# Where the router's slots, one power and the last 24 row scatters stand at the end of attention

## The chip, the cores and the metric

One core of a Trainium2 chip runs the whole layer. Its engines are TensorE (PE, matrix products), VectorE (DVE), ScalarE (ACT), GpSimd (POOL) and SyncE (SP, which issues loads and stores). Each works through its own program in order and waits on semaphores for the others. The metric is the device time of one execution in microseconds (us), the median of several runs.

## What is computed

A layer norm, linear attention, a residual sum, a second layer norm, and a mixture of experts with two of eight experts for each token, with a second residual sum. Of 8192 tokens (4 sequences of 2048) with 256 columns each:

```python
q = elu(x @ Wq + bq) + 1; k = elu(x @ Wk + bk) + 1; v = x @ Wv + bv      # 16 heads of 16
# for each position: s += k^T v; z += k; value = (q s) / (q z + 1e-6)
x = x + values @ Wo + bo
logits = einsum('th,eh->te', layernorm(x), router_w)
topk_logits, topk_idx = top_k(logits, 2); probs = softmax(topk_logits)
hmid = gelu(einsum('th,efh->etf', layernorm(x), w1) + b1)
y = einsum('etf,ehf->eth', hmid, w2) + b2
x = x + einsum('eth,te->th', y, combine)                                # combine holds probs
```

## The kernel before

**Blocks of attention.** The positions are cut into 16 blocks (STEPS) of 128, each for all four sequences. An iteration c works on several blocks at once: the front (projections and features) of block c, the attention of block c-1 (flag `bk`), the residual, second norm and router logits of block c-2 (flag `ro`), and the sending of the rows of block c-3 to the experts (flag `sc`). Iteration 16 (c == STEPS) has no front any more: it holds the attention of block 15, the last one. Iterations 17 and 18 have neither front nor attention. Iteration 17 closes the norm of block 15 and sends block 14; iteration 18 sends block 15.

**Sending rows.** For each token two rows of 260 numbers (1040 bytes: the normalised row, token number, two probabilities, first expert) go to `expert_in` in memory, at the row numbers in `cur`, its slots. `row_data` and `router_slots` make them on VectorE (L1405 to L1428); the last write to `cur` raises `slot_done`. GpSimd sends them with `scatter_one(b, t)` (L1801): one indirect DMA for 128 tokens of sequence b and choice t, 8 for a block. `scatter(b)` sends two. Blocks with even numbers count in the semaphore `scat_out[0]`, odd ones in `scat_out[1]`, 16 for each scatter that has landed, 128 for a block.

**The second norm.** `norm_moments` (VectorE, L1244) raises `ln2_ve`; GpSimd's `rstd` (L1769) takes the power -0.5 and raises `ln2_rs`; `norm2_shift` and `router_logits` on VectorE wait for that. In iterations up to 15 the moments come behind residual(r, 3), the slots behind score_lo(0, 3), and each of GpSimd's scatters stands alone between other work. In iteration 16 row_data stands ahead of attention(0), the moments behind state_part(0), the slots behind score_lo(1, 3), and GpSimd issues 2 scatters between state_add(0) and state_add(1) and 6 between state_add(2) and state_add(3).

**After attention.** VectorE adds up the experts' counts (`base`) and makes a table of tiles (`table`, L1632 to L1706, semaphore `tab`). SP then reads the table and loads the first tile's rows (`xg`, L556). The first loads wait for all scatters of even blocks, and of odd blocks only for those before block 15 if the first expert already has 1024 rows; the load of tile 4 (c == PRE) waits for all of them and for the padding rows that ScalarE sends (L1182). Meanwhile SP loads the second layer's weights, `w2raw`, in 8 loads of 512 KB, each behind the landing of the one before it. In the expert part TensorE turns the rows (L897), makes the hidden layer (pS, pO, pA) and the second layer (pU, pF); VectorE puts the result in `yt`, and GpSimd adds it to `out` with two scatters with addition for each tile (L1933). Those of one of the first tiles wait until those of the tile before have landed.

## Time and profile before

| | before |
|---|---|
| median of 3 runs | 1002.96 us |
| lowest, highest | 1000.09, 1008.81 us |
| profiled execution, time | 1012.54 us |
| profiled execution, span | 1010.8 us |
| PE, DVE busy share of the span | 91%, 74% |
| ACT, POOL busy share | 67%, 65% |
| mean granted TensorE clock | 0.973 of full speed |

The profiled execution is one run of its own: its time is 1.7 us more than its span, and 9.6 us above the median of the timed runs. Attention takes the span up to about 560 us, the expert part begins at about 595 us.

### The profile page before, as it was taken

The numbers are of one execution on the slowest core, as the hardware profiler recorded it, in microseconds if no ns is written. First come the engines' busy times: TensorE is split into PE (matmuls) and PEld (weight loads), VectorE is DVE, ScalarE is ACT, GpSimd is POOL, SyncE is SP. The second block draws the span as 40 slices with busy tenths as digits, with TensorE's granted clock in tenths as the row PEclk, the third lists the DMA queues.
The fourth block names the chain that finished last, engine by engine and source line by source line (L and its number), as shares of the span: only waits on it lengthen the run. The fifth ranks groups of instructions, "written<-read, shape, count | busy, mean of one in ns | idle before, by whom it ended". The sixth has DMA issues, their size and how long they took to land. (4 is left out here: it accounts for less than half of the span.)

```text
span 1010.8 us, 33673 instructions
## 1 busy us (share of the span) xinstructions
PE 917.7 (91%) x10722; PEld 739.2 (73%) x10723; DVE 753.0 (74%) x2280; ACT 674.2 (67%) x1295; POOL 652.9 (65%) x580
## 2 busy tenths in 40 slices
PE   6799899999999999999987569899999999999994
PEld 3577677767777777767766247678999999999994
DVE  6788698888898898888886565456666666666663
ACT  8868788888888988898874334444555555555552
POOL 3245868798788888898873444446565555656565
PEclk9999899999999999999999679999999999999998
DMA  6626744554556444644442654345555555555554
GB/s 181 205 74 193 247 137 152 176 159 142 153 156 185 130 151 147 181 154 138 143 143 88 200 179 76 64 80 87 99 87 95 93 92 97 89 99 89 98 87 50
DMA packets 103159, 131.31 MB, mean 130 GB/s; under 512 B 15120, under 2 KB 89360, under 8 KB 102736
## 3 DMA queue, kind: packets, MB, share of 16 engines
q1 hardware_dynamic: 74912, 92.54, 32.9%
q0 software_dynamic: 25680, 35.01, 18.7%
q10 hardware_dynamic: 2464, 2.38, 0.7%
q8 instruction: 64, 1.05, 0.5%
q14 instruction: 39, 0.32, 0.1%
HBM read 64.29 MB, written 65.60 MB: 129 GB/s over the span
## 5 line engine op out<-in xcount | busy, mean ns | idle before, releaser
L1933 POOL DMA_INDIRECT out<-yt,to_token x135 | 213.2, 1579 | 181.4 <-DVE yt L1760 81.8
L1285 DVE SCALAR_TENSOR_TENSOR ahl<-pS,ahl 128x512 f16<-128x512 f32 x240 | 161.4, 683 | 25.3 <-ACT ahl L992 22.3
L992 ACT ACTIVATE ahl<-pS 128x512 f16<-128x512 f32 x240 | 143.0, 603 | 45.2 <-PE pS L663 42.5
L1805 POOL DMA_INDIRECT expert_in<-xn,cur x128 | 131.4, 1027 | 35.9 <-issue 24.5
L1201 ACT ACTIVATE g<-pS,b1s 128x256 f32<-128x256 f32 (+1 forms) x140 | 57.2, 461 | 92.0 <-PE pS L573 92.0
L659 PE MATMUL pS<-cbs 128*128 128x384 bf16 x240 | 79.5, 331 | 21.9 <-DVE ahl L1285 17.7
L573 PE MATMUL pF<-xT,was 128*128 128x512 f16 x384 | 93.0, 379 | 6.1 <-DVE xT L1290 6.0
L573 PE MATMUL pS<-gT,w1s 128*128 128x256 f16 (+1 forms) x840 | 97.4, 272 | 1.2 <-issue 1.1
L1726 DVE TENSOR_TENSOR ghl<-g,ghl 128x1024 f16<-128x1024 f32 (+1 forms) x68 | 83.0, 1220 | 20.5 <-ACT ghl L1228 16.0
L573 PE MATMUL pF<-w2s,ghl 128*128 x816 | 95.4, 273 | 2.4 <-issue 1.6
L573 PE MATMUL pU<-w2s,ghl 128*128 x804 | 94.1, 273 | 1.8 <-issue 1.4
L663 PE MATMUL pS<-qst,kst 128*128 128x256 f16 x480 | 92.1, 274 | 0.0
L1799 POOL TENSOR_TENSOR state<-state,ut 128x272 f32<-128x272 f32 x64 | 49.8, 779 | 65.1 <-DVE ut L1324 64.3
L573 PEld LDWEIGHTS pS<-gT,w1s 128*128 x840 | 81.0, 99 | 13.0 <-issue 2.3
L684 PE MATMUL pO<-vhl,ahl 128*128 128x17 f16 x3072 | 87.8, 171 | 2.8 <-DVE ahl L1285 2.8
L684 PEld LDWEIGHTS pO<-vhl,ahl 128*128 128x128 f16 x3072 | 85.0, 96 | 6.0 <-DVE ahl L1285 3.8
L573 PEld LDWEIGHTS pF<-w2s,ghl 128*128 128x128 f16 x816 | 79.4, 98 | 13.0 <-issue 3.4
L573 PEld LDWEIGHTS pU<-w2s,ghl 128*128 128x128 f16 x804 | 78.2, 98 | 12.3 <-issue 2.8
L1201 ACT ACTIVATE g<-pO,b1s 128x256 f32<-128x256 f32 (+1 forms) x72 | 29.1, 458 | 77.9 <-PE pO L573 75.8
L1228 ACT ACTIVATE ghl<-g 128x1024 f16<-128x1024 f32 (+1 forms) x68 | 72.0, 1059 | 0.1
L573 PEld LDWEIGHTS pF<-xT,was 128*128 128x128 f16 x384 | 36.0, 98 | 40.4 <-DVE xT L1290 7.8
L663 PEld LDWEIGHTS pS<-qst,kst 128*128 128x128 f16 x480 | 47.2, 98 | 18.8 <-issue 0.5
(223 smaller groups left out, 2180.3 us busy)
## 6 DMA issues: line engine op xcount, KB each, us to landing
xg<-expert_in SPq DMA_DIRECT2D x64, 260.0 KB
qk_parts<-qkhl SPq DMA_DIRECT2D x64, 256.0 KB, 2.3
qst<-qk_parts SPq DMA_DIRECT2D x192, 64.0 KB
kst<-qk_parts SPq DMA_DIRECT2D x96, 128.0 KB
xs<-x SPq DMA_DIRECT2D x16, 512.0 KB, 4.7
out<-x SPq DMA_DIRECT2D x16, 512.0 KB, 3.2
w1raw<-w SPq DMA_DIRECT2D x16, 256.0 KB
w2raw<-w SPq DMA_DIRECT2D x8, 512.0 KB
```

What stands on the lines that cost most here:

```text
L573: mm = nc.tensor.matmul(out, lhs(a, k), rhs(b_, k), start=(t == 0), stop=(t == len(terms) - 1))
L659: nc.tensor.matmul(o[:].rearrange("p (h q) -> p h q", q=C)[:, :, 0:STACK], ident16, mask_first, start=True, stop=False, skip_group_check=True)
L663: mm = nc.tensor.matmul(o[:, e * 2 * C:(e + 1) * 2 * C], kst[:, sp_, pr, b * C:(b + 1) * C], qst[:, sp_, :, pr, b * C:(b + 1) * C], start= ...
L684: mm = nc.tensor.matmul(pO[:, h * VC:(h + 1) * VC], ahl[:, b % 2, a, h * C:(h + 1) * C], vhl[:, sp_, b_, b, h * VC:(h + 1) * VC], start=False,
L992: nc.scalar.activation(ahl[:, b % 2, 0, n * 4 * C:(n + 1) * 4 * C], score_bank(fr, n)[:], ACT.Relu).then_inc(sc_hi, 1)
L1201: nc.scalar.activation(g[:, p1, f, h * P:h * P + width], hidden[p1][f // 2][:, c0:c0 + width], ACT.Gelu, bias=b1s[:, bass.ds(e * FC + f, 1 ...
L1228: nc.scalar.activation(ghl[:, p1, 0, :, 0:n], g[:, p1, :, 0:n], ACT.Copy).then_inc(g_hi, 1)
L1285: V.scalar_tensor_tensor(ahl[:, b % 2, 1, cols], score_bank(fr, n)[:], 0.0, ahl[:, b % 2, 0, cols], ALU.max, ALU.subtract).then_inc(sc_lo, 1)
L1726: V.tensor_tensor(ghl[:, p1, 1, :, 0:n], g[:, p1, :, 0:n], ghl[:, p1, 0, :, 0:n], ALU.subtract).then_inc(g_lo, 1)
L1799: G.tensor_tensor(sb_, sb_, ut[:, b % 2], ALU.add).then_inc(state_new, 1)
L1805: G.indirect_dma_start(xg_dram, bass.IndirectOffsetOnAxis(ap=cur[:, qp, 2 * b + t:2 * b + t + 1], axis=0), xn2[:, qp, b], None).then_inc(s ...
L1933: G.indirect_dma_start(out, bass.IndirectOffsetOnAxis(ap=to_token[:, c % 2, s:s + 1], axis=0), yt[:, c % 2, s], None, compute_op=ALU.add). ...
```

## The change

Four edits. On VectorE, row_data, norm_moments, router_slots and norm2_shift of iteration 16 go to where the other iterations have them. On GpSimd, iteration 16 sends its 8 scatters singly between the state additions. In iteration 17, the power of block 15 (`rstd`) goes ahead of the first scatter of block 14. And of the last 16 scatters (blocks 14 and 15) each pair waits until the pair before it has landed.

```diff
-                if sc and c not in (STEPS, STEPS + 1):
+                if sc and c != STEPS + 1:
                     row_data()
...
-                if ro and c not in (STEPS, STEPS + 1):
+                if ro and c != STEPS + 1:
                     norm_moments(r, st2, mv2, ve2, (ln2_st, ln2_mv, ln2_ve))
...
-                if sc and c not in (STEPS, STEPS + 1):
+                if sc and c != STEPS + 1:
                     router_slots()
-                if ro and c not in (STEPS, STEPS + 1):
+                if ro and c != STEPS + 1:
                     norm2_shift()
...
-                if c == STEPS:
-                    row_data()
                 if bk:
                     attention(0)
                     state_part(0)
-                if c == STEPS:
-
-                    norm_moments(r, st2, mv2, ve2, (ln2_st, ln2_mv, ln2_ve))
...
-                if c == STEPS:
-                    router_slots()
-                    norm2_shift()
...
+                    if c > STEPS and t == 0 and b:
+
+                        pool.wait_ge(scat_out[qp], 128 * qh + 32 * b)
+                    if c > STEPS and t == 0 and b == 0:
+
+                        pool.wait_ge(scat_out[1 - qp], 128 * ((q + 1) // 2))
...
+                last = sc and c == STEPS
                 single = sc and c < STEPS
...
-                if c == STEPS + 1:
-                    scatter_one(0, 0)
                 if ro:
                     rstd(r, ve2, rs2, ln2_ve, ln2_rs)
                 if c == STEPS + 1:
-                    scatter_one(0, 1)
+                    scatter(0)
...
-                if sc and c in (STEPS, STEPS + 2):
+                if sc and c == STEPS + 2:
                     scatter(0)
                 if bk:
                     state_add(1)
-                if single:
+                if last:
+                    scatter_one(1, 1)
+                if single or last:
                     scatter_one(2, 0)
...
+                if last:
+                    scatter_one(3, 0)
-                if sc and c >= STEPS:
+                if sc and c > STEPS:
                     scatter(1)
                     scatter(2)
                     scatter(3)
```

GpSimd in iteration 16 before, from the power of block 14 to the first scatter of block 14 (`rs` is the power, `state` an addition for one sequence, `expert_in` a scatter):

```order
L1771 TENSOR_TENSOR rs<-ve,cfs 128x4 [waits ln2_ve]
L1799 TENSOR_TENSOR state<-state,ut 128x272 [waits o_ps,ut_done]
L1805 DMA expert_in<-xn,cur 69632x260 [waits slot_done]
L1805 DMA expert_in<-xn,cur 69632x260
L1799 TENSOR_TENSOR state<-state,ut 128x272 [waits o_ps,ut_done] x2
L1805 DMA expert_in<-xn,cur 69632x260 x6
L1799 TENSOR_TENSOR state<-state,ut 128x272 [waits o_ps,ut_done]
L1805 DMA expert_in<-xn,cur 69632x260 [waits slot_done]
```

The same stretch of GpSimd with the change, up to the second pair of block 14 in iteration 17:

```order
L1803 DMA expert_in<-xn,cur 69632x260 [waits slot_done]
L1791 TENSOR_TENSOR state<-state,ut 128x272 [waits o_ps,ut_done]
L1803 DMA expert_in<-xn,cur 69632x260 x2
L1791 TENSOR_TENSOR state<-state,ut 128x272 [waits o_ps,ut_done]
L1803 DMA expert_in<-xn,cur 69632x260 x2
L1791 TENSOR_TENSOR state<-state,ut 128x272 [waits o_ps,ut_done]
L1803 DMA expert_in<-xn,cur 69632x260 x2
L1791 TENSOR_TENSOR state<-state,ut 128x272 [waits o_ps,ut_done]
L1803 DMA expert_in<-xn,cur 69632x260
L1763 TENSOR_TENSOR rs<-ve,cfs 128x4 [waits ln2_ve]
L1803 DMA expert_in<-xn,cur 69632x260 [waits slot_done,scat_out1]
L1803 DMA expert_in<-xn,cur 69632x260
```

The runs of 2 and 6 scatters have become 1, 2, 2, 2 and 1, the power stands ahead of block 14's first scatter, and that scatter has a second wait. The six further pairs each wait for one of the two landing semaphores.

VectorE in iteration 16 with the change, between the residual of sequence 3 and the state part of sequence 0 (`ahl` is a score_lo, `mv` and `ve` the moments, L1419 to L1427 the slots, `sh` the shift):

```order
L1254 BN_STATS st<-x 128x6
L1248 BN_AGGR mv<-st 128x2 x4
L1250 TENSOR_REDUCE ve<-mv 128x4
L1285 SCALAR_TENSOR_TENSOR ahl<-pF,ahl 128x512
L1419 TENSOR_TENSOR pR<-pR,base 128x32
L1421 TENSOR_TENSOR sel<-oh,pR 128x64
L1426 TENSOR_REDUCE cur<-sel 128x8
L1427 TENSOR_TENSOR base<-pR,base 128x8
L1302 SCALAR_TENSOR_TENSOR sh<-mv,rs 128x4
L1285 SCALAR_TENSOR_TENSOR ahl<-pS,ahl 128x512
L1308 TENSOR_SCALAR rden<-pO 128x16
```

Before, only the two score_lo stood between the statistics and row_data; the moments came behind state_part(0), and the slots and the shift three score_lo later. No instruction is added or taken away on VectorE.

## Rows read from the trace of the kernel before

**Rows 1.** Windows by stage: us, busy time by engine, granted clock, DMA share, GB/s.

```profile
core 0: us, PE busy (x) PEld busy (x) DVE busy (x) ACT busy (x) POOL busy (x), PEclk, DMA share, GB/s
530.00:565.00 35.00, 22.42 (x340) 17.02 (x339) 22.01 (x82) 13.32 (x27) 12.10 (x14) 0.82 0.34 110
565.00:600.00 35.00, 23.22 (x95) 10.87 (x96) 24.01 (x101) 10.84 (x14) 21.07 (x18) 0.70 0.72 224
```

**Rows 2.** Timeline of VectorE: start, us, line, operation, [idle before, releaser].

```profile
541.20 0.17 DVE L1308 TENSOR_SCALAR rden<-pO 128x16 f32<-128x16 f32 x1 [1.88 <-remote]
...
559.65 0.17 DVE L1308 TENSOR_SCALAR rden<-pO 128x16 f32<-128x16 f32 x1 [7.68 <-remote]
```

**Rows 3.** Timeline of TensorE around the same two stretches and after them.

```profile
551.37 1.37 PE L684 MATMUL pO<-vhl,ahl 128*128 128x17 f16 x48 [0.64 <-DVE ahl L1285]
...
594.47 1.11 PE L897 MATMUL pF<-cfs,xg 128*128 128x128 f32 x4 [1.66 <-DMA xg<-expert_in]
...
615.28 0.38 PE L897 MATMUL pR<-cfs,xg 128*128 128x128 f32 x2
```

**Rows 4.** Timeline of GpSimd, attention's last blocks: start, issue time of each scatter.

```profile
516.31 0.96 POOL L1805 DMA_INDIRECT expert_in<-xn,cur  x1 [0.31 <-issue]
...
539.17 1.04 POOL L1805 DMA_INDIRECT expert_in<-xn,cur  x1 [1.69 <-DVE cur L1426]
540.51 0.96 POOL L1805 DMA_INDIRECT expert_in<-xn,cur  x1 [0.30 <-issue]
...
551.11 0.98 POOL L1805 DMA_INDIRECT expert_in<-xn,cur  x1 [0.15 <-issue]
...
557.46 0.97 POOL L1805 DMA_INDIRECT expert_in<-xn,cur  x1 [0.30 <-issue]
```

**Rows 5.** Timeline of VectorE, closing part: moments, slots, logits, sums, table.

```profile
566.31 0.16 DVE L1250 TENSOR_REDUCE ve<-mv 128x4 f32<-128x8 f32 x1
...
567.47 0.22 DVE L1426 TENSOR_REDUCE cur<-sel 128x8 int32<-128x64 f32 x1
...
570.77 0.19 DVE L1382 TENSOR_TENSOR lga<-lga,bor 128x32 f32<-128x32 f32 x1 [2.83 <-POOL rs L1771]
...
579.60 0.18 DVE L1679 TENSOR_TENSOR et<-et 128x24 f32<-128x24 f32 x1 [0.32 <-DVE et L1677]
...
584.58 0.16 DVE L1695 TENSOR_TENSOR et<-et 128x1 int32<-128x1 int32 x1 [1.06 <-DVE et L1692]
...
586.99 0.27 DVE L1706 CAST settled<-pU 1x128 int32<-1x128 f32 x1
```

**Rows 6.** Timeline of GpSimd, closing part: scatters and the last power.

```profile
568.62 0.98 POOL L1805 DMA_INDIRECT expert_in<-xn,cur  x1 [6.87 <-DVE cur L1426]
569.64 1.04 POOL L1771 TENSOR_TENSOR rs<-ve,cfs 128x4 f32<-128x4 f32 x1
...
579.53 0.96 POOL L1805 DMA_INDIRECT expert_in<-xn,cur  x1 [0.30 <-issue]
...
594.19 3.07 POOL L1805 DMA_INDIRECT expert_in<-xn,cur  x1 [0.30 <-issue]
```

**Rows 7.** Timeline of SP's queue: the loads of the first two expert tiles.

```profile
589.04 1.24 SPq L556 DMA_DIRECT2D xg<-expert_in  x2
```

**Rows 8.** Timeline of GpSimd, expert part: scatters with addition that wait for landings.

```profile
610.54 1.62 POOL L1933 DMA_INDIRECT out<-yt,to_token  x1 [13.08 <-DVE yt L1760]
612.47 2.42 POOL L1933 DMA_INDIRECT out<-yt,to_token  x1 [0.31 <-issue]
...
618.28 2.04 POOL L1933 DMA_INDIRECT out<-yt,to_token  x1 [3.19 <-DMA out<-yt,to_token]
...
627.08 1.54 POOL L1933 DMA_INDIRECT out<-yt,to_token  x1 [0.30 <-issue]
...
631.68 1.55 POOL L1933 DMA_INDIRECT out<-yt,to_token  x1 [2.86 <-DMA out<-yt,to_token]
```

**Rows 9.** DMA queues from 542 to 543 us: packets, MB, share.

```profile
q0 software_dynamic: 48, 0.13, 37.1%
```

More of the change, by code:

```diff
@@ L1852, in body @@
                     state_add(0)
-                if single:
+                if single or last:
                     scatter_one(0, 1)
@@ L1858, in body @@
                     low(3)
-                if single:
+                if single or last:
                     scatter_one(1, 0)
@@ L1868, in body @@
                     state_add(1)
-                if single:
+                if last:
+                    scatter_one(1, 1)
+                if single or last:
                     scatter_one(2, 0)
@@ L1872, in body @@
                     state_add(2)
-                if single:
+                if single or last:
                     scatter_one(2, 1)
-                if sc and c >= STEPS:
+                if last:
+                    scatter_one(3, 0)
+                if sc and c > STEPS:
                     scatter(1)
@@ L1884, in body @@
                     state_add(3)
-                if single:
+                if single or last:
                     scatter_one(3, 1)
```

## The prediction

> **What bounds the kernel now.** I read the windows by stage first, since the change touches only the seam between attention and the expert part. From 530 to 565 us TensorE is busy for 22.4 of 35 us and VectorE for 22.0; from 565 to 600 us TensorE for 23.2, at a mean granted clock of 0.70, while the DMA engines are at 0.72 [rows 1]. Neither engine is full here, so the seam is a chain of waits, and what counts is which wait ends last.
>
> Then the timelines, engine by engine. VectorE stands idle for 1.88 us before 541.20 and for 7.68 us before 559.65, both times ahead of attention's first instruction on pO, both with the releaser "remote" [rows 2]. TensorE's products for the second of them are recorded as done at 551.37 + 1.37 = 552.74 [rows 3], so the result is there 6.9 us before VectorE goes on. These are 9.6 us on the path. In the same two stretches GpSimd issues scatters one straight behind the other: two, at 539.17 and 540.51, and six, from 551.11 to 557.46 [rows 4]. That is the only thing that I find to tell these stretches from others.
>
> The closing part hangs on VectorE: the variances `ve` of block 15 are done at 566.31 + 0.16 = 566.47, which I call T. Block 14's slots are done at 567.69, the logits of block 15 start at 570.77 after 2.83 us idle for the power, and the table is done at 587.26. Between 579.1 and 584.6 there are five waits, the first and the last of them in the rows, of 0.32, 0.53, 0.88, 1.22 and 1.06 us [rows 5]: 4.0 us on tiny instructions, while scatters are being issued up to 583. The first two tile loads go out from 589.04 [rows 7], T + 22.6, and TensorE turns the second tile at 594.47 [rows 3]. From there TensorE and, from about 633 us, GpSimd's additions set the pace; the first addition starts at 610.54 when its `yt` is ready [rows 8]. All of this moves one for one with the first load.
>
> **The change, part by part.** The sum is made against the profiled execution, 1012.5 us.
>
> (1) Slots and moments of iteration 16. The same 15 small instructions, 0.16 to 0.22 us each by their kind [rows 5], move ahead of score_lo(1, 0) and leave later places. VectorE's total is the same, and it has 13 us of room in 35 [rows 1]. In return for up to 15 x 0.2 = 3 us early it gives back 3 us later; I take 0, with 0 to +1 as bounds. What it brings is that block 13's first scatter need not wait until 539.17 any more.
>
> (2) Scatters of iteration 16. Runs of 2 and 6 become 1, 2, 2, 2, 1. A single scatter costs GpSimd about 1 us of issue; nothing there waits for GpSimd. If runs of scatters make the remote waits, the 7.68 us go, and a run of two may still cost what it did at 539.17, 1.88 us. But two scatters that end at 516.31, also 1.3 us apart, have no such wait behind them [rows 4]. So of three runs of two I charge two, 3.8 us. Gain: 9.6 - 3.8 = 5.8 us. Bounds: 0 (other cause) and 9.6 (all goes).
>
> (3) Power ahead of the first scatter. It took place at 569.64, behind the scatter of 568.62 that itself waited 6.87 us for the slots [rows 6]. Ahead of it, it runs from T + 0.1 to T + 1.1, inside VectorE's own row_data and slots, and the logits start at about 568.0, not 570.77. That is 2.8 us off VectorE's chain. The first scatter still waits for the slots and keeps T + 2.15; its new wait, for block 13's last scatter, is over by then, since that one goes out with the last state addition, some us ahead of T.
>
> (4) Landed pairs. Before, block 14's eight scatters were issued from 568.62 to 579.53, and block 15's last at 594.19 [rows 6]. Now a pair costs P = 1.27 us to the second issue (six from 551.11 to 557.46, [rows 4]) plus the time until that one has landed. What a landing of a plain scatter takes, this trace doesn't show, since none is waited for. Upper neighbour: the scatters with addition, issued at 627.08 with the next one, which waits for its landing, at 631.68: 4.60 us; the addition's issue is 1.54 against 0.96 us, so I take 4.0, and P = 5.3 us. The longest of that kind is 612.47 to 618.28, 5.8 us [rows 8], P = 7.1. Lower bound: of the scatter issued at 540.51 all 48 packets run between 542 and 543 us [rows 9], so 2.5 us, P = 3.8. I stay near the additions, since weights, padding rows and scatters share the DMA engines here at 0.72 of their time.
>
> Who is behind the waits: on GpSimd the further pairs, then the additions of tile 0; on SP the first load, which needs all of block 14 landed, and tile 4's load, which needs block 15. Block 14 has landed at T + 2.15 + 4P = T + 23.4 (bounds 17.4 and 30.6). VectorE's chain alone would now allow the load at T + 22.6 - 2.8 = T + 19.8, or T + 15.8 if the five small waits go too. So the landing ends last, and parts (3) and the small waits are worth nothing: the first load goes out at T + 23.4, 0.8 us later than before. Only with P under (19.8 - 2.15)/4 = 4.4 us is anything of the power's 2.8 us left.
>
> GpSimd is free of scatters at T + 2.15 + 7P + 2.2 = T + 41.5; the first addition came at T + 44.1, so that is hidden with 2.6 us to spare. Block 15 has landed at T + 2.15 + 8P = T + 44.6. Tile 4 was turned at 615.28, T + 48.8 [rows 3], and a load takes about 5 us here (589.04 to 594.47), so it has to be issued by T + 43.8, or T + 44.6 after the shift: just in time. Its results have some more room, since GpSimd's additions set the pace by then.
>
> A rule speaks against part (4). The Trainium skill, "DMA: Bandwidth & Descriptors", section "Anatomy of one DMA — SWDGE (gpsimd) path", puts about 2 us of every such DMA down to setup and completion, whatever its size, and the wait for a landing lays it open eight times where back-to-back issue covers it. By its fit (2.0 us + bytes/436e3) a 133 KB scatter lands in 2.3 us, an estimate from that page; P would be 3.6 us, block 14 landed at T + 16.5, and VectorE's chain would decide with a gain of 2.8 us. No row here shows a landing that short, and the additions' 4.6 us speak against it.
>
> **Sum:** -5.8 (2) + 0.8 (4) + 0 (1, 3) = -5.0 us, so 1007.5 against 1012.5. The profiled execution is 9.6 us above the median of its timed runs, which spread over 8.7 us. That is as much as the remote waits, so they may well be smaller in many timed runs. I take 4 us off the median, not 5: 999 us.
>
> **The rivals.** *Nothing to win at the stalls.* The remote waits have another cause, or are mostly missing in timed runs (the lowest, 1000.1, may be one without them, and the 1.27 us pair at 516.31 had none). The closing chain had then no small waits either, the load stood at T + 18.6 in such a run, and the landings put it at T + 23.4: up to 4.8 us slower than the lowest run, against the median +1 to +5, about 1005. For it: the size of the gap between profile and timed runs. Against it: timed runs of 1003 and 1009 have something of 3 to 9 us in them.
>
> By the page "SBUF — State Buffer", section "Who interferes with whom", of the Trainium skill, TensorE and ScalarE wait for no one and a DMA never contends with a compute engine; by that rule scatters can't cause these waits, which is this rival. The coincidence with [rows 4] is why I give it less than my forecast.
>
> *Slower by landings.* If the landings take 5.8 us under load, P = 7.1, the first load goes out at T + 30.6, 8.0 us later, and block 15 has landed at T + 59, 15 us past T + 43.8, where tile 4's load has to go out, 7 of them beyond the shift. With the stalls unchanged that is +8 to +15, about 1013. It costs something from P = 5.1 (2.15 + 4P = 22.6) and outweighs the stalls' 5.8 us from P = 6.6.
>
> *Everything goes.* All 9.6 us of remote waits, landings under 4.4 us, and 2.8 us of the power: up to -12, with the time about 991.
>
> **How the numbers follow.** Forecast, 995 to 1002: 0.45. Nothing at the stalls, 1002 to 1009: 0.28. Slower by landings, above 1009: 0.12. Everything goes, below 995: 0.15. One per cent, 10 us, is about what a measurement of this kernel can tell from no change. Below 993 lies most of the last case, 0.12 in all; above 1013 half of the landings' case and a little more, 0.08. The rest is 0.80. The range 991 to 1010 leaves out about 1 in 10 on either side.
>
> **What the profile would show.** Right: no remote wait above 2 us in attention's last block; the logits of block 15 within 2 us of T; the first load released by a landing of `expert_in`, about 23 us behind T, with pairs on GpSimd 5.3 us apart. Wrong: a remote wait of several us beside a run of two scatters or beside none; pairs under 4.4 us apart, with the load behind the table; or TensorE waiting for tile 4's rows, or GpSimd's first addition directly behind its last scatter. The prediction fails above all if the timed runs of before hold no stall.

## The result: slower by 0.5 per cent

| | before | changed |
|---|---|---|
| median of 20 runs each | 1002.09 us | 1007.51 us |
| lowest, highest | 999.47, 1008.81 us | 1002.45, 1012.41 us |
| ratio, 95% interval | | 1.0053 [1.0038, 1.0067] |
| profiled execution, time | 1012.54 us | 1009.51 us |
| profiled execution, span | 1010.8 us | 1007.7 us |

The forecast was 999 us, and the time moved 5.4 us the other way. It lies in the range of 991 to 1010, at the place of the rival "nothing to win at the stalls" (about 1005). The two profiled executions by themselves show a gain of 3 us (forecast: 5). That the sum ends at 1007.5 us for the profiled execution and the timed median is 1007.51 us is chance. Why a trace and the timed runs can disagree in sign is the main finding of this case.

**What the profile after shows.** The busy shares and the mean clock hardly differ (PE 91%, DVE 75%, ACT 67%, POOL 64%; clock 0.978). The stages that answer to [rows 1], with the same columns:

```profile
530.00:565.00 35.00, 26.66 (x372) 19.06 (x371) 27.54 (x118) 15.07 (x28) 14.54 (x17) 0.90 0.40 125
565.00:600.00 35.00, 17.91 (x90) 10.90 (x88) 19.06 (x65) 11.50 (x18) 12.72 (x12) 0.71 0.62 194
```

The first window holds more work (VectorE 27.5 us, before 22.0), because the remote waits of [rows 2] are gone and attention ends earlier. The second holds less: TensorE 17.9 us, before 23.2; work has moved out of it into the first, and TensorE waits for the first load (last rows below).

VectorE after, the rows that answer to [rows 2] and [rows 5]: attention's first instruction on pO for sequence 3, the variances whose end is T, the logits and the sums of block 15, the table:

```profile
552.80 0.17 DVE L1308 TENSOR_SCALAR rden<-pO 128x16 f32<-128x16 f32 x1 [0.88 <-PE pO L684]
...
559.19 0.16 DVE L1250 TENSOR_REDUCE ve<-mv 128x4 f32<-128x8 f32 x1
...
560.79 0.19 DVE L1382 TENSOR_TENSOR lga<-lga,bor 128x32 f32<-128x32 f32 x1
...
566.99 0.16 DVE L1410 TENSOR_REDUCE pd<-one_exp 128x4 f32<-128x8 f32 x1 [3.22 <-ACT one_exp L1062]
...
575.95 0.27 DVE L1698 CAST settled<-pU 1x128 int32<-1x128 f32 x1
```

No remote wait is in this trace, T is 559.35 (before 566.47), the logits come at T + 1.4 without a wait for the power, and the table is done at 576.22, T + 16.9 (before T + 20.8). All of that is as the forecast had it or better, but it can't be put down to the change by this trace: series 1 shows that the kernel before has no remote waits either on some chips, and that this trace fits those. A new wait of 3.22 us stands ahead of the sums: ScalarE's exponentials for block 15 are late.

GpSimd after, the last scatter of block 13, the power, and the pairs of blocks 14 and 15 (answers to [rows 6]):

```profile
555.07 0.99 POOL L1803 DMA_INDIRECT expert_in<-xn,cur  x1 [0.16 <-issue]
559.44 1.04 POOL L1763 TENSOR_TENSOR rs<-ve,cfs 128x4 f32<-128x4 f32 x1 [3.38 <-DVE ve L1250]
561.51 1.04 POOL L1803 DMA_INDIRECT expert_in<-xn,cur  x1 [1.03 <-DVE cur L1426]
564.69 0.96 POOL L1803 DMA_INDIRECT expert_in<-xn,cur  x1 [2.15 <-issue]
569.91 0.96 POOL L1803 DMA_INDIRECT expert_in<-xn,cur  x1 [4.25 <-DMA expert_in<-xn,cur]
571.17 0.96 POOL L1803 DMA_INDIRECT expert_in<-xn,cur  x1 [0.30 <-issue]
574.28 1.23 POOL L1803 DMA_INDIRECT expert_in<-xn,cur  x1 [2.15 <-DMA expert_in<-xn,cur]
575.82 0.96 POOL L1803 DMA_INDIRECT expert_in<-xn,cur  x1 [0.30 <-issue]
580.00 1.58 POOL L1803 DMA_INDIRECT expert_in<-xn,cur  x1 [3.22 <-DMA expert_in<-xn,cur]
581.89 0.96 POOL L1803 DMA_INDIRECT expert_in<-xn,cur  x1 [0.31 <-issue]
585.29 0.95 POOL L1803 DMA_INDIRECT expert_in<-xn,cur  x1 [2.45 <-DMA expert_in<-xn,cur]
586.55 0.96 POOL L1803 DMA_INDIRECT expert_in<-xn,cur  x1 [0.30 <-issue]
593.93 0.96 POOL L1803 DMA_INDIRECT expert_in<-xn,cur  x1 [6.42 <-DMA expert_in<-xn,cur]
...
606.95 0.96 POOL L1803 DMA_INDIRECT expert_in<-xn,cur  x1 [0.30 <-issue]
608.95 1.62 POOL L1934 DMA_INDIRECT out<-yt,to_token  x1 [0.84 <-POOL to_token L1920]
```

SP's first load and TensorE's first turns after (answers to [rows 7] and [rows 3]):

```profile
585.32 1.57 SPq L556 DMA_DIRECT2D xg<-expert_in  x2
```

```profile
588.29 1.09 PE L897 MATMUL pR<-cfs,xg 128*128 128x128 f32 x4 [10.31 <-DMA xg<-expert_in]
591.12 1.12 PE L897 MATMUL pF<-cfs,xg 128*128 128x128 f32 x4 [1.74 <-DMA xg<-expert_in]
```

The load goes out at T + 26.0, in the same moment as the fifth pair on GpSimd (585.29), so both were released by the landing of block 14, 9 us after the table was done. SP's own waits between 555 and 600 us (engine and line, what it waited for: us in total, times, longest) say the same:

```profile
SPq L545 <- DMA expert_in<-xn,cur: 5.1, 1, 5.1
```

TensorE stands idle for 10.3 us ahead of the first turn (11.2 in e0 below, so most of that is not the change's). The first addition follows the last scatter directly, 0.84 us idle behind the tokens' copy: the reserve of 2.6 us is gone.

### The profile page after: what moved, and what is told of

The parts are those of the page before. It is cut to its first block, busy times and chain, and to the rows that moved or that the text cites. A ratio compares the mean times of both kernels' runs of the same rounds, so it can differ in the third digit from the quotient of the medians.

```text
span 1007.7 us, 33676 instructions
## 1 busy us (share of the span) xinstructions
PE 913.5 (91%) x10722; PEld 737.7 (73%) x10723; DVE 753.9 (75%) x2280; ACT 675.0 (67%) x1295; POOL 648.5 (64%) x580
## 4 chain that ended last, share of the span: by engine, by line
PE 43%; POOL 19%; DVE 10%; issue 9%; ACT 8%; DMA 7%; SPq 2%; POOLq 1%; DVEq 0%; ACTq 0%
PE pF L573 10%; PE pU L573 8%; PE pS L573 8%; PE pA L573 5%; POOL expert_in L1803 4%; PE pO L573 4%; DMA out<-yt,to_token 4%; POOL qf L1780 3%; POOL qkhl L1784 3%; POOL xs L1820 3%; ACT ahl L992 2%; PE pO L684 2%; POOL kf L1780 2%; DVE ahl L1285 2%; POOL state L1791 1%
## 5 line engine op out<-in xcount | busy, mean ns | idle before, releaser
L1934 POOL DMA_INDIRECT out<-yt,to_token x135 | 211.0, 1563 | 170.1 <-DMA out<-yt,to_token 80.9
L1803 POOL DMA_INDIRECT expert_in<-xn,cur x128 | 129.0, 1008 | 50.3 <-DMA expert_in<-xn,cur 24.8
L1718 DVE TENSOR_TENSOR ghl<-g,ghl 128x1024 f16<-128x1024 f32 (+1 forms) x68 | 82.9, 1220 | 20.8 <-ACT ghl L1228 20.8
L573 PEld LDWEIGHTS pS<-gT,w1s 128*128 x840 | 80.9, 99 | 12.8 <-issue 2.3
L573 PEld LDWEIGHTS pU<-w2s,ghl 128*128 128x128 f16 x804 | 78.1, 98 | 12.8 <-issue 3.2
```

Source lines behind the costliest of these rows:

```text
L573: mm = nc.tensor.matmul(out, lhs(a, k), rhs(b_, k), start=(t == 0), stop=(t == len(terms) - 1))
L1718: V.tensor_tensor(ghl[:, p1, 1, :, 0:n], g[:, p1, :, 0:n], ghl[:, p1, 0, :, 0:n], ALU.subtract).then_inc(g_lo, 1)
L1803: G.indirect_dma_start(xg_dram, bass.IndirectOffsetOnAxis(ap=cur[:, qp, 2 * b + t:2 * b + t + 1], axis=0), xn2[:, qp, b], None).then_inc(s ...
L1934: G.indirect_dma_start(out, bass.IndirectOffsetOnAxis(ap=to_token[:, c % 2, s:s + 1], axis=0), yt[:, c % 2, s], None, compute_op=ALU.add). ...
```

## The experiments

They were run in five series, each on a chip of its own with its own runs of before, so ratios compare within a series. The medians of before in them were 1002.7, 1010.5, 1011.6, 1004.5 and 1004.3 us. All kernels compute the whole layer. Times written T + ... are read from rows of their traces.

### Series 1: which part costs

**e0_before** is the kernel before, profiled once more.

> The kernel before, unchanged, profiled a second time. Theory A (the remote waits of 1.88 and 7.68 us were an accident of the first profiled execution and the timed runs mostly lack them): no remote wait above 2 us, the variances of block 15 done near 559 us, and the first tile load near 579 to 582 us, 19.5 to 22 us behind them. Theory B (runs of scatters make them in every execution): a wait of several us ahead of the last pO again, and the first tile load near 588.

Its one execution took 1006.56 us. Its trace has no remote wait on VectorE at pO, although its runs of two and six scatters stand where they stood. VectorE's first instruction on pO for sequence 3, which waited 7.68 us at 559.65 [rows 2], in e0:

```profile
548.66 0.17 DVE L1308 TENSOR_SCALAR rden<-pO 128x16 f32<-128x16 f32 x1 [0.88 <-PE pO L684]
```

GpSimd in e0: the first and the last of the run of six that lies over it, the first and the eighth scatter of block 14, and the last of block 15:

```profile
546.92 0.98 POOL L1805 DMA_INDIRECT expert_in<-xn,cur  x1 [0.15 <-issue]
...
553.26 0.97 POOL L1805 DMA_INDIRECT expert_in<-xn,cur  x1 [0.30 <-issue]
557.37 0.99 POOL L1805 DMA_INDIRECT expert_in<-xn,cur  x1 [2.34 <-DVE cur L1426]
...
568.27 0.96 POOL L1805 DMA_INDIRECT expert_in<-xn,cur  x1 [0.30 <-issue]
...
580.86 0.96 POOL L1805 DMA_INDIRECT expert_in<-xn,cur  x1 [0.30 <-issue]
```

The run starts 1.6 us ahead of the end of TensorE's products in e0 (546.92 against 548.55) and in the trace of before (551.11 against 552.74, [rows 3, 4]): the same program at the same distance, once with a wait of 7 us and once without. T is 555.22 here, the first load goes out at T + 22.3, and the last two of the eight loads of weights stand ahead of it in SP's program:

```profile
570.16 4.53 SPq L423 DMA_DIRECT2D w2raw<-w  x2
577.49 1.73 SPq L556 DMA_DIRECT2D xg<-expert_in  x2
```

The table was done at 572.66, T + 17.4, and block 14 has landed at 571.02, T + 15.8, by the trace's record of landings, 2.75 us behind the issue of its eighth scatter. So neither of them holds the first load here. SP itself does: each load of weights waits for the landing of the one before, the last is out at 574.69, and SP then reads its row numbers (L531 to L540), 2.8 us in all. Its wait for block 14 (L545) lasts 17 ns.

**e1_no_landing_waits**: the changed kernel without part (4).

```diff
-                    if c > STEPS and t == 0 and b:
-                        pool.wait_ge(scat_out[qp], 128 * qh + 32 * b)
-                    if c > STEPS and t == 0 and b == 0:
-                        pool.wait_ge(scat_out[1 - qp], 128 * ((q + 1) // 2))
```

> The changed kernel without the two landing waits; the rest as changed. Theory A (the landing waits hold up the first tile load by 26.0 us behind the variances where the table would allow about 19): this is 5 to 8 us faster than the changed kernel, 1000 to 1002 us, ratio to the kernel before 0.998 to 1.001, and the first load leaves 19 to 20 us behind the variances. Rival (the moved slots and single scatters of iteration 16 cost the time): it stays at 1006 to 1008, ratio 1.004 or more.

Measured: 1.0012 [0.9993, 1.0032], so parts (1) to (3) together bring nothing that can be told from noise. The first load leaves at T + 22.4, not at 19 to 20: SP's last load of weights went out at 579.28, T + 18.7, and the first tile load 3.4 us behind its end.

**e2_landing_waits_alone**: before with just those four lines added.

> The kernel before with the landing waits alone; power, slots and single scatters as before. Theory A: ratio 1.004 to 1.007, with the first load 25 to 27 us behind the variances. Rival (the waits are harmless, the loss is in iteration 16): 0.998 to 1.002.

Measured: 1.0025 [1.0012, 1.0038]. The landing waits alone make the kernel slower by 2.5 us. That is less than theory A had (4 us at least), though the first load stands where it had it: at T + 26.7 against T + 22.3, and the first addition at T + 50.5 against T + 46.7. 1.7 us of this is a later start: the first scatter of block 14 goes out at T + 3.8, not T + 2.15, since it waits for the landing of the run of six.

**e3_power_alone**: before with part (3).

```diff
-                if c == STEPS + 1:
-                    scatter_one(0, 0)
                 if ro:
                     rstd(r, ve2, rs2, ln2_ve, ln2_rs)
                 if c == STEPS + 1:
-                    scatter_one(0, 1)
+                    scatter(0)
```

> The kernel before with the power of block 15 ahead of block 14's first scatter, nothing else. The prediction's 2.8 us on VectorE's chain, if the table is what the first load waits for: 999 to 1000.5 us, ratio 0.997 to 0.999. Rival (another wait takes its place: ScalarE's second weight pass ahead of block 15's probabilities waits for its DMA, 3.2 us on VectorE in the changed kernel; or block 14's landings end last): ratio 0.999 to 1.002.

Measured: 1.0014 [0.9995, 1.0032], no gain. VectorE in e3 at the logits and the sums of block 15:

```profile
560.17 0.19 DVE L1382 TENSOR_TENSOR lga<-lga,bor 128x32 f32<-128x32 f32 x1 [1.69 <-DMA expert_in<-xn,cur]
...
565.91 0.16 DVE L1410 TENSOR_REDUCE pd<-one_exp 128x4 f32<-128x8 f32 x1 [2.77 <-ACT one_exp L1062]
```

In e0 these two waits were 2.83 us (for the power) and 1.27 us. The power is done at 558.14 in e3; the logits then wait for the landing of block 13's run of six, which the kernel asks for ahead of them (`scat_out[rp]`). What is gained at the first wait is lost at the second, because ScalarE, ahead of block 15's exponentials, waits for a load of weights:

```profile
563.23 1.91 ACT L1170 ACTIVATE w2s<-w2raw 128x2048 f16<-128x2048 f32 x1 [6.69 <-DMA w2raw<-w]
565.04 0.84 ACT L1062 ACTIVATE one_exp<-mx 128x1 f32<-128x1 f32 x4
```

The first load goes out at T + 22.1, again 2.8 us behind SP's last load of weights, so an earlier table would not have helped it either.

### Series 2: on a chip where the remote waits are there

Before took 1010.5 us here, 8 us more than in the first series, and the traces of e4, e6 and e7 show the remote waits again. The kernel before itself has no trace on this chip or on that of series 3.

**e4_vector_part_alone**: part (1) without the rest.

> The kernel before with VectorE's edit alone: row_data, moments, slots and shift of iteration 16 at the places of the other iterations. From block 12's last scatter (seven or eight us ahead of iteration 16's power) to the variances of block 15 the profiles so far show 28.0 us with the old places and 30.1 with the new ones. Theory A (VectorE's edit makes these 2.1 us, since TensorE's products with pO wait for score_lo behind it): 30.1 us again, ratio 1.001 to 1.004. Rival (GpSimd's single scatters make them): 28.0 us and ratio 0.999 to 1.001.

Measured: 1.0001 [0.9983, 1.002]. The wait of 1.88 us is gone, since the run of two now goes out at 538.33, ahead of VectorE's instruction at 542.32. The long one stays, at 560.16 with 7.69 us. From block 12's last scatter to T this trace takes 36.9 us, so the 28.0 and 30.1 us of the expectation, read where no remote wait was, decide nothing here.

**e5_single_scatters_alone**: part (2) without the rest (the single scatters as in the diff of the change; slots, moments, power and landings as before).

> The kernel before with GpSimd's single scatters of iteration 16 alone; slots and power as before. Theory A: 28.0 us over the same stretch, ratio 0.999 to 1.001, at most +0.5 us for the first state addition behind a scatter that waits for late slots. Rival (the scatters between the state additions hold up attention): 29 us or more.

Measured: 0.9938 [0.9917, 0.9959], 6.3 us faster. VectorE in e5 at the same two places:

```profile
541.07 0.17 DVE L1308 TENSOR_SCALAR rden<-pO 128x16 f32<-128x16 f32 x1 [1.21 <-PE pO L684]
...
554.06 0.17 DVE L1308 TENSOR_SCALAR rden<-pO 128x16 f32<-128x16 f32 x1 [2.15 <-PE pO L684]
```

The two waits are 1.21 and 2.15 us, with TensorE as the releaser, not 1.9 and 7.7 us with something remote. They are shorter, not gone: TensorE's products are recorded as done at 540.17 and 552.69, 0.9 and 1.4 us before VectorE goes on, where e0 has 0.1 us or less. From block 12's last scatter to T e5 takes 31.4 us, the trace of before 37.2 and e0 28.0. So 5.8 us of the 9.2 go and 3.4 stay. The theory written for e5 (28.0 us, no gain) failed; the prediction's part (2), 5.8 us with 3.8 us left, holds on this chip.

**e6_block15_in_landed_pairs**: before with landing waits in iteration 18 alone.

```diff
+                    if c == STEPS + 2 and t == 0 and b:
+                        pool.wait_ge(scat_out[qp], 128 * qh + 32 * b)
```

> The kernel before with landing waits only between block 15's pairs; block 14's eight scatters straight behind each other. Theory A (the waits cost at block 14, which holds up the first tile load, and help behind it, because the load then has the DMA engines more to itself): first load 22 us behind the variances as before, landed 1.5 to 4 us sooner than in the kernel before, last scatter near 40 us behind the variances, ratio 0.996 to 1.000. Rival (the last scatters come too late for tile 4, or the additions queue behind them): ratio 1.002 or more.

Measured: 1.0006 [0.9983, 1.0028], nothing that can be told from before. The landing waits of block 15 alone show no cost here, up to the 2.8 us that the interval leaves open; those of block 14 are ahead of the first load. Its trace also gives one more pair of rows for the long wait, VectorE's end of it and the start of the last scatter of the run of six:

```profile
561.48 0.17 DVE L1308 TENSOR_SCALAR rden<-pO 128x16 f32<-128x16 f32 x1 [7.64 <-remote]
```

```profile
559.29 0.97 POOL L1807 DMA_INDIRECT expert_in<-xn,cur  x1 [0.30 <-issue]
```

The issue ends at 560.26 and VectorE goes on 1.22 us later. In the traces of before, e4 and e7 it is 1.22 us as well (558.43 to 559.65, 558.94 to 560.16, 559.20 to 560.42). Beside a run of two VectorE goes on 0.27 us ahead of its end (541.47 and 541.20 in before). So these waits end at a fixed distance from the end of the run of scatters, not with any work of VectorE's own chain.

**e7_power_and_probabilities_first**: e3, and ScalarE takes block 15's probabilities ahead of that conversion of weights.

```diff
+                if c == STEPS + 2:
+                    w2_high(1)
...
-                    w2_high(1)
```

(The call moves from iteration 17 to behind `top_probability` in iteration 18.)

> The kernel before with the power first and, on ScalarE, block 15's probabilities ahead of the second weight pass that waits for its DMA. Theory A (the first load waits for block 14's landings, about 22.2 us behind the variances, not for the table): the table comes 14 to 15.5 us behind the variances instead of 17.5, the load stays at 22 +- 0.7, ratio 0.998 to 1.001. Rival (the table is what counts): the load comes 2 us or more sooner, ratio 0.996 to 0.998.

Measured: 0.9989 [0.997, 1.0009]. The table is done at T + 14.1, 6.7 us earlier than in [rows 5], but the first load goes out only at T + 20.9. Of 6.7 us on the chain of VectorE 1.7 us reach the load. Here SP's loads of weights are out at T + 12.2, and of block 14's 128 records of landings this trace has 27, the last at T + 17.3; SP has a remote wait of its own, 1.4 us at L540. What holds the load in e7 stays open.

### Series 3: the change and its best parts on such a chip

**f1_changed_again** is the changed kernel, **f4_changed_without_vector_part** is the changed kernel with slots and moments in the old places, **f2_singles_power_probabilities** puts e5 and e7 together (parts (2) and (3) and ScalarE's move, without (1) and (4)).

> The changed kernel, unaltered, on the chip of this job. Two groups of chips have shown up: one on which the kernel before has remote waits of 1.9 and 7.7 us in attention's last block in every profile (its median there 1010.5 us), one on which it has none (1002.7 us). Theory A (the result depends on the chip's kind): where before is near 1010, the changed kernel is faster, ratio 0.994 to 0.999; where before is near 1002.5, ratio 1.003 to 1.007 as in the first comparison. Rival (the changed kernel loses about 5 us everywhere): 1.003 or more on either.

> The changed kernel with VectorE's edit undone: slots and moments of iteration 16 at their old places, single scatters, power first and landing waits kept. Theory A (VectorE's edit costs 2.1 us of attention's last block): 1 to 3 us faster than the changed kernel, ratio 0.001 to 0.003 below its ratio. Rival (the first load waits for landings anyway, and hides it): the same as the changed kernel within 1 us.

> The kernel before with the single scatters of iteration 16, the power first, and on ScalarE block 15's probabilities ahead of the second weight pass; no landing waits, VectorE's slots at their old places. Theory A: no remote wait above 3 us on either kind of chip, 28 to 31 us from block 12's last scatter to the variances; where before is near 1010, ratio 0.992 to 0.995; where it is near 1002.5, ratio 0.998 to 1.001. Rival (the first tile load behind block 14's landings takes back the single scatters' gain): 0.997 or more where before is near 1010.

Measured against before at 1011.6 us: the change 0.9971 [0.9951, 0.9991], without its VectorE part 0.9944 [0.9924, 0.9964], and f2 0.9903 [0.9881, 0.9925]. On this chip the very kernel that lost 0.5% wins 0.3%. Parts (1) and (4) eat up most of the gain: by the ratios it is 2.7 us faster without part (1) (by the medians 1.7, 1006.65 against 1008.31 us; the runs of f1 and f4 alone barely tell the two apart), and 6.9 us faster without (1) and (4) and with ScalarE's move (by the medians 5.3). f2 gains more than expected (0.992 to 0.995), and at 1003.1 us it is as fast as before is on the chips without the waits.

**f3_run_of_six_behind_attention**: before, but the run of six behind the last state addition.

```diff
-                if sc and c >= STEPS:
+                if sc and c > STEPS:
                     scatter(1)
                     scatter(2)
                     scatter(3)
...
+                if sc and c == STEPS:
+                    scatter(1)
+                    scatter(2)
+                    scatter(3)
```

> The kernel before with the run of six scatters moved behind the last state addition, so that it runs beside the end of attention instead of beside TensorE's last products with pO. Theory A (VectorE's remote wait lasts until 1.2 us behind the end of the run, whatever it stands beside, when a result of TensorE is wanted during it; chips with the waits only): the 7.7 us wait goes from attention(3), and a wait of several us stands in the closing chain instead. Rival (only the many small products of attention are held up): no wait above 3 us anywhere. On a chip without the waits this says nothing of them, and the ratio is 0.999 to 1.002.

Measured: 0.9969 [0.995, 0.9987]. VectorE in f3, the instruction beside the run of two, that for sequence 3, and the logits of block 15:

```profile
538.22 0.17 DVE L1308 TENSOR_SCALAR rden<-pO 128x16 f32<-128x16 f32 x1 [1.94 <-remote]
...
550.65 0.17 DVE L1308 TENSOR_SCALAR rden<-pO 128x16 f32<-128x16 f32 x1 [0.88 <-PE pO L684]
```

```profile
565.73 0.19 DVE L1382 TENSOR_TENSOR lga<-lga,bor 128x32 f32<-128x32 f32 x1 [7.06 <-DMA expert_in<-xn,cur]
```

The long remote wait has gone with the run of six, which starts at 552.91 now, and the short one beside the run of two has stayed. That ties each wait to its run. What is won is partly paid for at the logits, 7.06 us: the power is done at 562.56, and the logits wait on for the landing of block 13's last scatter, issued at 559.26, as they did in e3. So this trace doesn't say whether a run there would have made a remote wait, which theory A was about. Shorter remote waits do stand in the closing part on this kind of chip, 1.87 us at 580.29 here, 2.65 us in e7 and 2.20 us in f2.

### Series 4: once more where the waits are missing

**g1_f2_again**, **g2_changed_third** and **g3_single_scatters_again** repeat f2, the change and e5; **g4_run_of_eight** joins the runs of two and six:

```diff
-                if sc and c in (STEPS, STEPS + 2):
+                if sc and c == STEPS + 2:
                     scatter(0)
...
+                if sc and c == STEPS:
+                    scatter(0)
```

> The kernel of f2 (single scatters, power and probabilities first, no landing waits) unaltered. Theory A: where the kernel before is near 1002.5 us (no remote waits) the ratio is 0.996 to 1.001, where it is near 1011, 0.988 to 0.993. Rival (its gain is that of the remote waits and its first load comes too late without them): 1.002 or more where before is near 1002.5.

> The changed kernel, unaltered. Theory A: ratio 1.003 to 1.007 where before is near 1002.5, 0.995 to 0.999 where it is near 1011. Rival (the two comparisons so far differ by chance and not by the chip's kind): near 1.001 on either.

> The kernel before with single scatters in iteration 16 alone. Theory A: 0.998 to 1.001 where before is near 1002.5, since there is no wait to remove; 0.992 to 0.996 where it is near 1011.

> The kernel before with all eight scatters of block 13 in one run between state_add(2) and state_add(3), none ahead of state_add(1). Theory A (a run of scatters beside attention's last products holds their semaphore back until 1.2 us behind the run's end, on the chips of the one kind): no wait near 1.9 us, one of 7.7 + 2.5 = 10.2 us ahead of attention(3), ending 1.2 us behind the last scatter, and a ratio of 1.000 to 1.002. Rival (the wait has a length of its own): 7.7 us again. On a chip of the other kind: no remote wait in either case, ratio 0.999 to 1.002.

Measured against before at 1004.5 us: f2 1.0004 [0.9985, 1.0022], the change 1.006 [1.004, 1.008], single scatters 1.0004 [0.9985, 1.0024], the run of eight 1.0012 [0.9996, 1.0029]. None of the four traces has a remote wait at pO, not even g4's beside eight scatters. So g4 couldn't tell whether the wait would grow with the run; it says that on this chip even a run of eight holds up nothing at pO. Single scatters, worth 6 us in series 2, are worth nothing here, and the change loses again.

### Series 5: the loss in two halves

> Part (1) alone, slots and moments of iteration 16 in the other iterations' places, everything else as before. My theory has two conditions. On a chip without remote waits the stage from block 12's last scatter to the variances of block 15 takes 30.1 us instead of 28.0, since TensorE's products on pO wait 1.95 us for a score_lo, and the whole is slower by 2.1 us, ratio 1.002. On a chip with them part of it lies under the wait of 7.7 us, and the ratio is 1.000 as in e4. The rival: the 2.1 us of the stage are given back later (the first load is bound by landings there), so the ratio is 1.000 on either kind.

> The changed kernel with slots and moments in their old places. On a chip without remote waits my theory has only the landing waits left of what costs time, as in e2: ratio 1.0025 (1.001 to 1.004), against 1.005 to 1.006 for the whole change. On a chip with remote waits 0.994 as in f4. The rival, that the old places cost nothing and the landing waits the whole 5 us: 1.005 on a chip without remote waits.

**h1_vector_part_again** (e4's kernel) 1.0011 [0.9988, 1.0033], **h2_changed_without_vector_part_again** (f4's) 1.0024 [1.0004, 1.0045], before at 1004.3 us, and again no remote wait in either trace. h2 comes out as the theory has it: without its VectorE part the change loses what the landing waits lose alone (e2: 1.0025), not 1.005 to 1.006. h1 can't tell the theory's 1.002 from the rival's 1.000. Its stage is longer as in the changed kernel, with the same row on TensorE:

```profile
533.83 1.40 PE L684 MATMUL pO<-vhl,ahl 128*128 128x17 f16 x48 [1.95 <-DVE ahl L1285]
```

## Why the prediction was wrong

**The step that failed is (2), or rather whose 9.6 us they were.** "These are 9.6 us on the path" was read from one execution whose time was 9.6 us above the median, and the sum took 4 us off that median. There are two kinds of chip, or of job, since each chip served one series only. On two (series 2 and 3; before 1010.5 and 1011.6 us) the waits are in the traces of the kernels that keep the old runs of scatters (e4, e6, e7, f3). On three (series 1, 4 and 5; before 1002.7 to 1004.5 us) they are in none. Before at 1002.09 us in the comparison fits the second kind, its trace with 1012.54 us the first. The trace of the changed kernel was taken in one of the 20 timed runs (1009.51 us), and it is of the second kind: VectorE waits 0.88 us at pO for sequence 3, as in e0, e1, g2 and h1, against 2.26 us for the same kernel in f1, and the stretch from block 12's last scatter to T takes 30.1 us, as in e1, against 31.5 in f1. So the timed runs were made where the waits are missing; for those of before that rests on their time. Subtracting the two profiled executions compares two chips besides two kernels.

The mechanism was right where it exists (e5, -6.3 us against -5.8), and absent where the time was measured. That the size agrees so well is in part luck: what stays in e5 is 0.9 and 1.4 us behind TensorE's products and some delay of TensorE, not two waits of 1.9 us. The prediction named stalls missing from the timed runs as what would make it fail above all, and still charged 4 of 5 us. Its argument against the rival, that timed runs of 1003 and 1009 us must hold something, fails too: in series 1 before spreads from 999.3 to 1007.4 us with no such wait in any trace. An excess of the profile over the median that equals a stall is a warning that the stall may be missing in the median, not a proof (the profiled execution of e1 is 6.0 us above its median without any such wait); half of it had to go to the rival.

**(4), right in its place, too small in its size.** The landing of block 14 releases the first load, as forecast, and not the table. It came at T + 26.0, not T + 23.4. The first scatter stood at T + 2.16 (forecast 2.15). The four pairs took 8.4, 4.4, 5.7 and 5.3 us, a mean of 5.95 for P = 5.3. From the second issue to the landing they took 5.2, 3.1, 4.2 and 3.4 us, a mean of 4.0, just what was taken from the additions. The mis-sized part is the other one, 1.27 us from the first to the second scatter: they were 3.18, 1.26, 1.54 and 1.89 us, a mean of 1.97. By the trace's record of landings the shortest in this trace is 2.4 us (the last scatter of all), the shortest of block 14 2.85. The Trainium skill, "DMA: Bandwidth & Descriptors", section "Anatomy of one DMA — SWDGE (gpsimd) path", gives 2.3 us by its fit, an estimate that the shortest landings come near and the others don't. That waiting for landings costs time is borne out by e2 and h2.

**The baseline of (4) left out SP's own program.** The prediction let the first load wait for the table or for block 14's landing. A third thing stands ahead of it: SP issues the eight loads of weights first, each behind the landing of the one before. In the trace of before they were out at T + 12.8, because the remote waits had made T late, and the load followed the table by 1.8 us. Without remote waits the last is out at T + 19.5 (e0), later than the table (T + 17.4) and than block 14's landing (T + 15.8), and the load goes out at T + 22.3. In e0, e1, e3, g1, g3, g4 and h1 the load stands 2.5 to 3.4 us behind the end of that issue, and SP waits for no landing of `expert_in`; it waits for one, for 5.1 to 6.5 us, only in the six traces with block 14's landing waits (changed, e2, f1, f4, g2, h2). That is why an earlier table buys nothing: in g1 it is done at T + 13.2 and the load goes out at T + 21.6. The rival had put the load at T + 18.6 for such a run. Block 14's eight scatters back to back had landed at T + 15.8 in e0 and T + 18.4 in e1, its four waited pairs at T + 25.7, and part of that difference only fills time in which SP was busy with the weights. The load is 3.7 us later in the changed kernel than in e0, and the measured price is 2.5 us (e2) and 2.4 us (h2), for which +0.8 was charged. That the loads of weights hold the first load is read from rows; no run moved them.

**GpSimd's reserve.** "Hidden with 2.6 us to spare" failed. GpSimd was free of scatters at T + 48.6 (607.91), 7.1 us later than T + 41.5: 2.6 us from block 14's four pairs and 4.5 from the three of block 15, which took 8.6, 5.4 and 6.3 us. The first addition follows at T + 49.6; in e0 it stood at T + 46.7. The fifth pair's landing, 7.4 us from 586.55, falls on the tile loads of 585.32 and on a 1 MB load that SP issues at 586.93. How much of the 2.5 us comes from the first load and how much from here isn't separated. e6, with block 15's landing waits alone, showed no loss on a chip with remote waits, to within 2.8 us.

**(1) was taken as 0 with +1 as its bound; its stage is 2.1 us longer.** From the start of block 12's last scatter to T the old places take 28.0 us in e0, e2 and e3 (527.24 to 555.22 in e0), the new ones 30.1 in the changed kernel (529.25 to 559.35) and in e1, 29.8 in h1. TensorE in the changed kernel and in before at sequence 0's products on pO:

```profile
533.80 1.38 PE L684 MATMUL pO<-vhl,ahl 128*128 128x17 f16 x48 [1.95 <-DVE ahl L1285]
```

```profile
532.25 1.37 PE L684 MATMUL pO<-vhl,ahl 128*128 128x17 f16 x48 [0.37 <-DVE ahl L1285]
```

The moments stand ahead of the score_lo for which these products wait. Windows of 2 us over the place, before:

```profile
532.00:534.00 2.00, 1.75 (x56) 1.69 (x57) 1.47 (x8) 0.62 (x2) 0.00 (x0) 1.00 0.77 262
...
536.00:538.00 2.00, 1.44 (x18) 1.26 (x18) 1.97 (x6) 0.78 (x3) 1.48 (x2) 1.00 0.04 8
538.00:540.00 2.00, 2.00 (x60) 1.92 (x59) 1.24 (x5) 1.19 (x2) 0.83 (x1) 1.00 0.00 0
```

and of the changed kernel:

```profile
532.00:534.00 2.00, 0.20 (x8) 0.20 (x9) 1.66 (x9) 0.60 (x2) 0.76 (x1) 1.00 0.64 224
...
536.00:538.00 2.00, 1.80 (x8) 1.22 (x9) 1.60 (x4) 1.28 (x3) 1.49 (x3) 0.50 0.19 67
538.00:540.00 2.00, 2.00 (x19) 1.55 (x18) 1.38 (x2) 0.86 (x2) 1.43 (x2) 0.66 0.22 75
```

TensorE is busy for 0.20 us of two where it had 1.75, and behind that the granted clock is 0.50 (1.2 GHz, the lower of its two levels) from 536 to 538 us and 0.66 in the next two, where before had 1.00 in these windows. The other traces with the new places (e1, e4, f1, g2, h1) fall to between 0.50 and 0.56 in one window of 2 us here, those of e0, g1 and h2 with the old ones stay at 1.00. The step asked whether VectorE had room in 35 us (13 us) and not which of its instructions TensorE waits for next. That the longer stage reaches the end is shown in part: with the rest of the change beside it, part (1) makes 1.0060 out of 1.0024 (g2 and h2, two chips) and 0.9971 out of 0.9944 (f1 and f4, one chip), 3.6 and 2.7 us by the ratios, neither far outside the noise; alone it gave 1.0001 and 1.0011, both open towards 2 us.

**(3) right in its place, worth nothing, but only half for the reason given.** In the changed kernel the landing did hide it; in e3 and e0 it was SP's loads of weights, which end later than the table. Besides, 2.8 us at the logits became a wait of 2.8 us (e3) or 3.2 us (changed) for ScalarE, which the chain as read didn't contain, since VectorE's wait there was 1.3 us or less before.

**The sum on a chip without waits**: 2.1 (1) + 0 (2) + 0 (3) + 2.5 (4) = 4.6 us, measured 5.4 and 6.0. The 2.1 us are the length of the stage, not a measured price. The parts come from several chips, and none of the traces can place the last microsecond: from T to the end of the span they take between 440.7 us (e7) and 449.6 us (e0), a spread larger than the effect. So the late first load and the late first addition are seen, and their price is known from timed runs alone.

**The rivals.** "Nothing to win at the stalls" is what happened, in its second form (the waits are missing in the timed runs), with part (1) on top. It was right that the five small waits before the table are missing then too (table at T + 17.4 in e0). "Slower by landings" has a share: a mean pair of 5.95 us is past the 5.1 us from which it costs. On three chips no wait of VectorE at pO goes with a run of scatters; on two it does, and is shorter where the run is split (e5) or gone when it is elsewhere (f3). The rule of the Trainium skill, "SBUF — State Buffer", section "Who interferes with whom", that a DMA never contends with a compute engine agrees with the first three and doesn't explain the other two. The prediction made more of it than it says, since the same section names a pair of ports that VectorE and GpSimd share: it speaks against the transfers as the cause, not against GpSimd's own work at issuing them. No run here tells these two apart.

## What to carry to other kernels

When the profiled execution is longer than the median by as much as one stall in it, suspect that the timed runs lack the stall, price the change both with it and without, and if a second trace can be had, take it first. List everything that stands ahead of a load in its own queue's program: here the first tile load was held by SP's loads of weights as soon as T came early, and two candidates on other engines were moved in vain. Putting the first tile load ahead of the last loads of weights is the obvious next step, and wasn't tried. A wait for landings is paid on whichever load needs the last of them: find the first consumer, and split the price of a pair into issue and landing, since either can grow. And before moving "free" small instructions on an engine with room, look for the one instruction behind them that TensorE is waiting for: 1.6 us of new idle time there cost the lower clock besides.

The version to keep is f2: 0.9903 [0.9881, 0.9925] on a chip with the waits, 1.0004 [0.9985, 1.0022] on one without.

## What the runs showed of the hardware

- Chips differ, or the jobs on them, since each chip served one series: five of them gave before medians of 1002.7, 1004.3, 1004.5, 1010.5 and 1011.6 us, and the two with the longest times are those whose traces have VectorE waiting for 1.9 us beside a run of two scatters and 7.7 us beside one of six. Why they differ stays open, as does what VectorE waits for: the releaser is recorded only as "remote".
- The waits end at a fixed distance from the end of a run (1.22 us behind a run of six, in four traces; 0.2 to 0.3 us ahead of the end of a run of two, in before, e6, e7 and f3). Where the six are split, in e5, f1, f2 and f4, VectorE goes on 0.8 to 0.9 us behind the pair beside sequence 3, 1.3 to 1.5 us after TensorE's products are recorded as done (0.1 us in e0).
- Where the waits are, the record of landings has gaps where scatters go out in a run (26 of block 14's 128 in before, 27 in e7), and is whole for block 14 where pairs wait for each other (f1, f4). In e0, without the waits, it is whole too. What that has to do with the waits is open.
- The second scatter of iteration 17 starts 3.2 us behind the first, with the power between them (e0: 3.24) or without (3.18, of which 2.15 us idle with nothing recorded), and 3.4 us in g4 and 6.9 in f3, where block 13's run ends right before the first. That is why moving the power doesn't bring the scatters forward. Its cause is open.
- A scatter of 133 KB lands 2.4 to 7.8 us after its issue starts, in the traces with a whole record. It took 2.75 us for the last of block 14's eight back to back in e0, 7.8 us for the last of block 15 there, with tile loads beside it, and 2.4 us for the last in the changed kernel.
